# Two mixture-of-experts layers of a decoder: a streamed sort in the last one, and sorted expert tiles in the top-2 one

## The chip, the cores and the metric

The kernel runs on one core of one Trainium2 chip. The time is device microseconds of that core, from one execution; the number compared is the median over several executions. Each kernel also has one execution taken by the hardware profiler, whose span runs from the first to the last instruction.

## What is computed

Two decoder layers over 32 sequences of 128 tokens with 128 features (4096 tokens), all in float32: a bidirectional Mamba block, a cross attention, a top-2 mixture of experts; then a windowed attention, a cross attention and a top-1 mixture of experts. The change is in the two mixtures. The first, cut to what matters:

```
xt = layernorm(x).reshape(-1, 128);  logits = xt @ gate_w.T            # 8 experts
_, idx = top_k(logits + beta, 2);    probs = sigmoid(logits at idx)
c = zeros((4096, 8)).at[rows, idx].add(probs)
eo = for each expert: (silu(xt @ gate_e) * (xt @ up_e)) @ down_e       # inner width 256
x = x + sum_e c[:, e] * eo[:, e] + the same with the shared expert, weight 1
```

The last one: each token goes to the expert with the largest router logit, `gelu(x @ W1[e] + b1[e])` (inner width 512), then one common output matrix, the residual and a layernorm with its own gamma and beta.

## The kernel before

The six parts run one after the other; each has a block in which the five engines run their own lists of instructions and meet through semaphores. The tokens stay on chip in `S.x`, 128 tokens of a sequence on the partitions, and are worked on in `NG` = 8 groups of `GS` = 4 sequences (512 tokens). A part that needs weights of the next one issues their loads on SP's queue at its own start (`ahead.load(sp)`, L163).

**Top-2 layer** (`moe_top2_layer`, tiles named `c_`). A first block normalises all tokens (POOL's ten-step `ln_scalars`, then DVE), transposes them (L1301), forms the router's logits (L1305), splits the tokens and the expert weights into two parts `hi` and `lo` (L1322, L1325, L1381, L1392), and finds the two best experts of all 4096 tokens in one row of DVE steps (L1348 to L1379). A second block then runs every token through all 9 experts (8 and the shared one): 8 groups times 9 experts are 72 units. A unit is 4 projections of 128x512, each as three matmuls on the split parts (`split_pass`, L181 to L183), two Silu of 128x512 on ACT (L1465), two products on DVE (L1479), 8 output matmuls of 128x128 (L1443), and the weighted sum on DVE (L1503, L1505), where the weight is zero for the experts that a token did not choose.

**Top-1 layer** (`moe_top1_layer`, tiles named `f_`). A first block does the same preparation for all 4096 tokens (L1922, L1927, L1966), finds each token's expert, counts the tokens by expert with two matmuls and a scan, and works out each token's place in a sorted table in which each expert starts at a multiple of `TILE` = 256 (L1981 to L2025). Only then does POOL send the rows: 32 indirect DMAs, one for a sequence (L2048), into the DRAM table `f_sorted`, whose 6144 rows of 400 numbers were filled with blank rows beforehand. That fill is one DMA of 9600 KB, the last part of `moe_top1_weights`, issued on SP by the cross attention ahead of it:

```python
    blank = w["blank"].unsqueeze(0).to_broadcast([NT * TILE // 128, 128, ROW])
    W.part(W.sorted.rearrange("(j p) c -> j p c", p=128), blank)
```

A second block runs 24 tiles of 256 sorted tokens. For a tile SP loads the rows (L2078), PE transposes them (L2091) and multiplies by the one expert that the tile needs (L2101; ACT has copied its matrix, L2132, at an address read from the table `expert`) and by the output matrix (L2110), ACT does the Gelu (L2140), DVE the layernorm (L2151 to L2183), and POOL sends the rows to their tokens' places in the output with two indirect DMAs (L2206). ACT reads all 24 entries of `expert` ahead of its first tile (L2125).

The cross attention ahead of the top-1 layer loads for each sequence its context and mask on SP (L986, L993) a few sequences ahead, behind whatever SP issued before.

Of the kernel before, what the change touches and what calls it, by code (L numbers as in the profile page):

```python
# [24 lines left out]
GS = 4  # L25
# [1224 lines left out]

def moe_top2_weights(nc, ctx, w):
    W = Weights(nc, ctx, "cw_")
    W.router = W.tile("router", [128, E0], w["router"])
    W.bias = W.tile("bias", [128, E0], w["bias"].partition_broadcast(128))
    W.order = W.tile("order", [128, E0], w["order"].partition_broadcast(128))
    W.gu = W.tile("gu", [128, E0 + 1, 2, M0], w["gu"])
    W.down = W.tile("down", [128, E0 + 1, M0 // 128, D], w["down"])
    return W


def moe_top2_layer(nc, S, W, ahead):

    NE, MC = E0 + 1, M0 // 128
    BELOW = -1.0e38  # L1270
    with ExitStack() as ctx:
        A = Alloc(nc, ctx, "c_")
        gu_hi, gu_lo = (A.sb(n, [128, NE, 2, M0], F32R) for n in ("gu_hi", "gu_lo"))
        xh = [A.sb(f"xh{p}", [128, GS, D]) for p in range(2)]
        xT = [A.sb(f"xT{p}", [128, GT]) for p in range(2)]
        x_hi, x_lo = (A.sb(n, [128, NG, GT], F32R) for n in ("x_hi", "x_lo"))
        logits, sigm, sel, best, first, second, c = (
            A.sb(n, [128, NB, E0]) for n in ("logits", "sigm", "sel", "best", "first", "second", "c"))
        top, pick = A.sb("top", [128, NB]), A.sb("pick", [128, NB])
        with ExitStack() as ctx1:  # L1280
            B = Alloc(nc, ctx1, "c1_")
            pt = [B.ps(f"pt{k}", [128, GT]) for k in range(2)]
            pl = B.ps("pl", [128, NB, E0])
            s = {n: B.sem(n) for n in """rstd xh_ready t_mm xT_ready hi_ready lo_ready l_mm gu_hi_ready
                gu_lo_ready l_ready sigm_ready route""".split()}
            with nc.Block() as block:

                @block.sync
                def _(sp):
                    ahead.load(sp)  # L1290

                @block.tensor
                def _(pe):
                    pe.wait_ge(W.loaded, W.all())

                    def body(g, p):
                        pe.wait_ge(s["xh_ready"], g + 1)
                        if due(g - 1):
                            pe.wait_ge(s["xT_ready"], g - 1)
                        for i in range(GS):  # L1300
                            ins = nc.tensor.transpose(pt[p][:, i * T:(i + 1) * T], xh[p][:, i, :], S.ident[:, :])  # L1301
                        ins.then_inc(s["t_mm"], 1)
                        pe.wait_ge(s["xT_ready"], g + 1)
                        for i in range(GS):
                            ins = nc.tensor.matmul(pl[:, bass.ds(g * GS + i, 1), :], xT[p][:, i * T:(i + 1) * T],  # L1305
                                                   W.router[:, :], start=True, stop=True)
                        ins.then_inc(s["l_mm"], 1)
                    walk_groups(pe, body)

                @block.scalar  # L1310
                def _(act):
                    A_ = nc.scalar.activation

                    def body(g, p):
                        act.wait_ge(s["t_mm"], g + 1)
                        if due(g - 1):
                            act.wait_ge(s["l_mm"], g - 1)
                        if due(g - 1):
                            act.wait_ge(s["lo_ready"], g - 1)
                        A_(xT[p][:, :], pt[p][:, :], ACT.Copy).then_inc(s["xT_ready"], 1)  # L1320
                        act.wait_ge(s["xT_ready"], g + 1)
                        A_(x_hi[:, bass.ds(g, 1), :], bc(xT[p][:, :], 1, 1), ACT.Copy).then_inc(s["hi_ready"], 1)  # L1322
                    walk_groups(act, body)
                    act.wait_ge(W.loaded, W.all())
                    A_(gu_hi[:, :, :, :], W.gu[:, :, :, :], ACT.Copy).then_inc(s["gu_hi_ready"], 1)  # L1325
                    act.wait_ge(s["l_ready"], 1)
                    A_(sigm[:, :, :], logits[:, :, :], ACT.Sigmoid).then_inc(s["sigm_ready"], 1)

                @block.vector
                def _(dve):  # L1330
                    V = nc.vector
                    dve.wait_ge(s["rstd"], LN_STEPS)

                    def body(g, p):
                        if isinstance(g, int) and g == 1:
                            dve.wait_ge(s["rstd"], 2 * LN_STEPS)
                        if due(g - 1):
                            dve.wait_ge(s["t_mm"], g - 1)
# [46 lines left out]
                def _(pool):  # L1385
                    for part, cols in enumerate(LN_PARTS):
                        S.ln_scalars(pool, s["rstd"], LN_EPS, cols, part * LN_STEPS)
# [485 lines left out]
def moe_top1_layer(nc, S, W, out_d):  # L1873
# [9 lines left out]
    with ExitStack() as ctx:  # L1883
# [182 lines left out]
        def real(j):  # L2066

            return 0 <= j < NT
# [243 lines left out]
```

## Time and profile before

| | us |
|---|---|
| median of 3 runs | 2602.59 (2600.07 to 2607.44) |
| the profiled execution's own time | 2606.87 |
| its span, first to last instruction | 2605.1 |
| busy in the span: PE, DVE, ACT, POOL | 2228.4, 1960.4, 1402.3, 1305.2 |
| top-2 layer in the span | 1226.8 to 1610.1 |
| cross attention of the second layer | 2128.4 to 2393.3 |
| top-1 layer | 2393.9 to 2605.1 |

The shares of busy time are means over parts with different limits, so the table is only a frame: a part that changes is read in its own stretch. A row of the timeline gives the start, the duration, the engine, the line and the operation, and in brackets how long the engine had stood idle and what ended that.

### The profile page before, as it was taken

The numbers are of one execution on the slowest core, as the hardware profiler recorded it, in microseconds if no ns is written. First come the engines' busy times: TensorE is split into PE (matmuls) and PEld (weight loads), VectorE is DVE, ScalarE is ACT, GpSimd is POOL, SyncE is SP. The second block draws the span as 40 slices with busy tenths as digits, with TensorE's granted clock in tenths as the row PEclk, the third lists the DMA queues.
The fourth block names the chain that finished last, engine by engine and source line by source line (L and its number), as shares of the span: only waits on it lengthen the run. The fifth ranks groups of instructions, "written<-read, shape, count | busy, mean of one in ns | idle before, by whom it ended". The sixth has DMA issues, their size and how long they took to land. (4 is left out here: it accounts for less than half of the span.)

```text
span 2605.1 us, 45217 instructions
## 1 busy us (share of the span) xinstructions
PE 2228.4 (86%) x14292; PEld 1469.1 (56%) x14292; DVE 1960.4 (75%) x2979; ACT 1402.3 (54%) x2570; POOL 1305.2 (50%) x947
## 2 busy tenths in 40 slices
PE   4888888888888877998699997799999986998267
PEld 1344333334343335776588886566666654776266
DVE  5999999999999994776455555688888864777235
ACT  4666776665766644664322222566666643664044
POOL 4878887778887773333100002355555531233636
PEclk7999999999999998999699999899999987998589
DMA  4222222222222222001000000000000024000232
GB/s 119 74 75 73 75 72 70 76 70 75 76 74 70 73 65 67 12 11 27 1 1 1 0 0 6 1 0 0 0 0 0 0 82 124 12 12 5 92 116 78
DMA packets 79274, 116.20 MB, mean 45 GB/s; under 512 B 29124, under 2 KB 42611, under 8 KB 78464
## 3 DMA queue, kind: packets, MB, share of 16 engines
q1 hardware_dynamic: 75072, 105.76, 13.6%
q0 software_dynamic: 3584, 8.66, 0.9%
q8 instruction: 47, 0.77, 0.1%
q10 hardware_dynamic: 512, 0.53, 0.1%
q14 instruction: 59, 0.48, 0.1%
HBM read 105.73 MB, written 20.05 MB: 48 GB/s over the span
## 5 line engine op out<-in xcount | busy, mean ns | idle before, releaser
L858 POOL TENSOR_TENSOR m_hc<-m_h,m_cs 128x1024 f32<-128x1024 f32 x256 | 603.0, 2360 | 185.8 <-DVE m_h L768 167.6
L768 DVE TENSOR_TENSOR_SCAN m_h<-m_da,m_pdb 128x1024 f32<-128x1024 f32 x256 | 585.3, 2286 | 27.8 <-DVE m_pdb L740 3.9
L461 PE MATMUL m_py<-m_hc,ident 128*128 128x512 f32 x1024 | 508.9, 621 | 1.9 <-POOL m_hc L858 1.9
L643 ACT ACTIVATE m_da<-m_dt,m_aneg 128x508 f32<-128x508 f32 x512 | 331.9, 709 | 118.2 <-DVE m_h L768 102.6
L740 DVE TENSOR_TENSOR m_pdb<-m_du,m_pdb 128x1024 f32<-128x1024 f32 x256 | 309.1, 1208 | 29.4 <-PE m_pdb L448 20.3
L461 PEld LDWEIGHTS m_py<-m_hc,ident 128*128 128x128 f32 x1024 | 200.8, 199 | 225.2 <-issue 216.7
L1833 POOL TENSOR_TENSOR d_pr<-d_pr,d_rden 128x512 f32<-128x512 f32 x128 | 133.3, 1041 | 177.4 <-DVE d_rden L1764 177.4
L1465 ACT ACTIVATE c_act_of<-c_pg 128x512 f32<-128x512 f32 x144 | 86.2, 598 | 237.5 <-PE c_pg L183 237.5
L1111 ACT ACTIVATE x_prT<-x_pt 77x512 f32<-77x512 f32 x256 | 137.9, 587 | 132.1 <-PE x_pt L1013 131.2
L448 PE MATMUL m_pdb<-m_bcrow,m_sel 96*128 96x512 bf16 x256 | 102.0, 399 | 110.2 <-DVE m_h L768 110.2
L1227 POOL TENSOR_TENSOR x_kd<-x_kT,x_hm 128x308 f32<-128x308 f32 x64 | 45.1, 705 | 300.5 <-ACT x_v_raw L1123 300.5
L118 POOL TENSOR_TENSOR t<-bn 128x4 f32<-128x4 f32 (+1 forms) x4 | 1.0, 240 | 356.7 <-POOLq L66 356.5
L448 PEld LDWEIGHTS m_pdb<-m_bcrow,m_sel 96*128 96x128 bf16 x256 | 25.7, 100 | 227.4 <-DVE m_h L768 178.7
L1843 POOL TENSOR_TENSOR d_r<-d_mean_sq,minus_half 128x20 f32<-128x20 f32 x32 | 113.1, 3534 | 73.7 <-DVE d_mean_sq L1790 73.6
L1479 DVE TENSOR_TENSOR c_h<-c_act_of,c_pu 128x512 f32<-128x512 f32 x144 | 98.3, 687 | 63.4 <-PE c_pu L183 45.7
L1443 PEld LDWEIGHTS c_pd<-cw_down,c_h 128*128 128x128 f32 x1152 | 139.5, 191 | 5.5
L1443 PE MATMUL c_pd<-cw_down,c_h 128*128 128x128 f32 x1152 | 139.9, 275 | 0.0
L1013 PE MATMUL x_pt<-ident,x_pr 128*77 128x128 f32 x1024 | 139.4, 280 | 0.2
L1013 PEld LDWEIGHTS x_pt<-ident,x_pr 128*77 128x77 f32 x1024 | 117.7, 150 | 27.5 <-issue 24.8
L1600 PE MATMUL d_ps<-d_kT,d_qT 128*128 128x256 f32 x512 | 133.1, 383 | 0.0
L407 PE MATMUL m_pm<-m_xnT,m_wtap 128*128 128x512 f32 x256 | 124.2, 609 | 1.3 <-ACT m_xnT L558 1.3
L1173 DVE TENSOR_REDUCE x_top<-x_ps 128x8 f32<-128x616 f32 x128 | 101.9, 796 | 27.2 <-PE x_ps L1032 11.9
(269 smaller groups left out, 4895.4 us busy)
## 6 DMA issues: line engine op xcount, KB each, us to landing
m_cs<-crow SPq DMA_DIRECT2D x256, 256.0 KB, 3.1
f_sorted<-in_F_blank SPq DMA_DIRECT2D x1, 9600.0 KB, 39.3
f_row<-f_sorted SPq DMA_DIRECT2D x24, 400.0 KB, 3.5
cw_gu<-in_C_gu SPq DMA_DIRECT2D x1, 2304.0 KB
x<-in_x SPq DMA_DIRECT2D x8, 256.0 KB, 4.5
fw_w<-in_F_w SPq DMA_DIRECT2D x1, 2048.0 KB, 9.6
bm_mrow<-in_B_mrow SPq DMA_DIRECT2D x1, 1232.0 KB, 7.9
x_ctxT<-in_B_ctxT SPq DMA_DIRECT2D x32, 38.5 KB, 1.8
```

Source lines behind the costliest of these rows:

```text
L407: ins = mm(pm[1 - c][:, :], wtap[:, d, k, c * 128:(c + 1) * 128], xnT[:, par[0], :, off:off + T], start=k == 0, stop=k == TAPS - 1)
L448: mm(pdb[:, row_bank(n), :], sel[:, n, :], bcrow[d][:, :], start=True, stop=True).then_inc(s["b_mm"], 1)
L461: ins = mm(py[:, c, :], S.ident[:, :], hc[n % BUF][:, c, :], start=False, stop=n == NS - 1)
L643: A_(dst, src, ACT.Exp, scale=aneg[:, d, c, n:n + 1]).then_inc(s["da_ready"], 1)
L740: V.tensor_tensor(out, du[d][:, ::-1, :], bc(pdb[:, row_bank(n), :], 1, CH), ALU.mult).then_inc(s["db_ready"], 1)
L768: V.tensor_tensor_scan(h[n % BUF][:, way], da[n % BUF][:, d:d + CH * GT][:, way], pdb[:, b:b + 2, :].rearrange("p c t -> p (c t)")[:, way] ...
L858: P.tensor_tensor(hc[n % BUF][:, :, :], h[n % BUF][:, :].rearrange("p (c t) -> p c t", c=CH), bc(cs[n % BUF][:, :], 1, CH), ALU.mult).then ...
L1013: ins = tr(pt[e][0:TC, i * T:(i + 1) * T], pr[u.p][u.h][:, QH * e + i, :], S.ident[:, :])
L1111: A_(prT[u.p][Q2 * u.h + e][:, :], pt[e][0:TC, :], ACT.Copy).then_inc(s["prT_ready"], 1)
L1443: ins = mm(pd[k][:, i, :], h[k][:, c_, i * T:(i + 1) * T], W.down[:, e, c_, :], start=c_ == 0, stop=c_ == MC - 1)
L1600: ins = mm(ps[q % 2][:, 2 * k:2 * k + 2, :], qT[b.p][:, 2 * q + k, :], kT[b.p][:, q, :, :], start=False, stop=k == 1)
L1833: P.tensor_tensor(pr[qd][:, :, :], pr[qd][:, :, :], bc(rden[qd][:, :], 2, T), ALU.mult).then_inc(s["norm_ready"], 1)
```

## The change

1. **Top-1 layer, sort.** One block in place of two, and everything is done group by group: ACT normalises a group (with scale and shift, L2291) and copies its transpose, DVE adds the two residual columns (`fill`, before on POOL), chooses, and ranks the group against running counts (`rank`), and POOL sends the group's 4 sequences at once. To know a place before all tokens are counted, each expert has a region of its own, `REGION` = 4352 rows, in the DRAM table. The 9600 KB fill is gone; after the last group SP writes 256 blank rows behind each expert's last row (8 DMAs of 400 KB, at addresses read from `tail_at`), and reads each tile's address from `tile_at`. ACT reads the entries of `expert` one by one, two tiles ahead.
2. **Top-2 layer.** The same streamed sort, with rows of 144 numbers (128 features, and for each expert the weight and the destination), each token sent twice (64 indirect DMAs). During the sort the shared expert is computed densely: per group 4 plain float32 projections of 128x512, 2 Silu, 2 products, 8 output matmuls, one add into `S.x`. Then 40 tiles of 256 rows, each with its own expert's matrices (one copy of 128x768 on ACT), two indirect DMAs of the weighted rows into the DRAM table `c_routed`, and at the end 8 groups are read back, two tables of 256 KB each, and added to `S.x` (L109 statistics as before). The three-matmul split is gone: all matmuls are plain float32.

The other four parts are unchanged. The core of the diff:

```diff
-    W.gu = W.tile("gu", [128, E0 + 1, 2, M0], w["gu"])
-    W.down = W.tile("down", [128, E0 + 1, M0 // 128, D], w["down"])
+    W.gud = W.tile("gud", [128, E0 + 1, 3 * M0], w["gud"])
+    W.sorted = nc.dram_tensor("c_sorted", [E0 * REGION + TILE, ROW0], F32).ap()
+    W.routed = nc.dram_tensor("c_routed", [K0 * NB * T, D], F32).ap()
...
+                group(0)
+                logits(0)
+                for g in range(NG):
+                    shared(g, 0)
+                    if g + 1 < NG:
+                        group(g + 1)
+                    count_up(g)
+                    shared(g, 1)
+                    if g + 1 < NG:
+                        logits(g + 1)
+                    shared_down(g)
...
+                def weigh(g):
+                    act.wait_ge(r["raw_ready"], g + 1)
+                    into = rows[:, g * GS:(g + 1) * GS, D:ROW0].rearrange("p b (e w) -> p b e w", w=2)
+                    A_(into[:, :, :, 0], logit[:, :, :], ACT.Sigmoid).then_inc(r["sig_ready"], 1)
...
+                    if real(j + 1):
+                        e, k = e_of[j + 1], (j + 1) % KW
+                        A_(bc(wt[k][:, :], 1, 1), W.gud[:, bass.ds(e, 1), :], ACT.Copy).then_inc(s["w_ready"], 1)
...
+                for g in range(NG):
+                    choose(g)
+                    shared(g, 0)
+                    rank(g)
+                    if g + 1 == NG:
+                        tables()
+                    shared(g, 1)
+                    shared_add(g)
...
+                for g in range(NG):
+                    dve.wait_ge(routed_in[g % 2], 16 * K0 * (g // 2 + 1))
+                    V.tensor_tensor(seqs(S.x, g), seqs(S.x, g), back_in[g % 2][:, 0], ALU.add).then_inc(s["half_ready"], 1)
...
+                    for b in range(g * GS, (g + 1) * GS):
+                        for k in range(K0):
+                            P.indirect_dma_start(W.sorted, bass.IndirectOffsetOnAxis(slot_of[:, k, b:b + 1], 0),
+                                                 rows[:, b, :], None).then_inc(sorted_in, 16)
...
-    W.sorted = nc.dram_tensor("f_sorted", [NT * TILE, ROW], F32).ap()
-    blank = w["blank"].unsqueeze(0).to_broadcast([NT * TILE // 128, 128, ROW])
-    W.part(W.sorted.rearrange("(j p) c -> j p c", p=128), blank)
+    W.blank = w["blank"]
+    W.sorted = nc.dram_tensor("f_sorted", [E1 * REGION + TILE, ROW], F32).ap()
...
+                for e in range(E1):
+                    at = sp.value_load(tail_at[0:1, e:e + 1], min_val=e * REGION, max_val=e * REGION + NB * T)
+                    sp.dma_start(W.sorted[bass.ds(at, TILE)], W.blank).then_inc(blank_in, 16)
...
-                e_of = [act.value_load(expert[0:1, j:j + 1], min_val=0, max_val=E1 - 1) for j in range(NT)]
```

SP's queue in the second cross attention, where the loads for the top-1 layer stand between the context loads of the first two sequences and those of the third (`x_ctxT`, `x_mask`). Before:

```order
L986 DMA x_ctxT<-in_E_ctxT 128x77
L993 DMA x_mask<-in_E_mask 128x77
...
L163 DMA fw_w<-in_F_w 128x4096
L163 DMA fw_wo<-in_F_wo 128x512
L163 DMA f_sorted<-in_F_blank 48x4x12800
...
L986 DMA x_ctxT<-in_E_ctxT 128x77
```

And now:

```order
L163 DMA fw_beta<-in_F_beta 128x128
L163 DMA fw_w<-in_F_w 128x4096
L163 DMA fw_wo<-in_F_wo 128x512
L997 UNCONDITIONAL_BRANCH
...
L986 DMA x_ctxT<-in_E_ctxT 128x77
...
L993 DMA x_mask<-in_E_mask 128x77
```

The fill of `f_sorted` no longer stands ahead of the third sequence's context.

PE in the top-2 layer of the changed kernel: first a group of the sort (`c_gT` is the group's transpose, `c_ones` and `cw_above` count), then a tile (`c_wt` holds the tile's expert):

```order
L1413 MATMUL c_pg<-c_gT,cw_gud 128x512
L1414 MATMUL c_pu<-c_gT,cw_gud 128x512
L1384 MATMUL c_pt<-ident,c_rows 128x128 x4
L1402 MATMUL c_pu<-c_chosen,c_ones 128x32
L1403 MATMUL c_pu<-c_chosen,cw_above 128x32
L1413 MATMUL c_pg<-c_gT,cw_gud 128x512
L1414 MATMUL c_pu<-c_gT,cw_gud 128x512
L1392 MATMUL c_pg<-cw_router,c_gT 128x8 x4
L1423 MATMUL c_pd<-cw_gud,c_sh_h 128x128 x8
...
L1446 MATMUL c_pt<-ident,c_row 128x128 x2
L1463 MATMUL c_pg<-c_xT,c_wt 128x256 x2
L1468 MATMUL c_pu<-c_xT,c_wt 128x256 x2
```

A group holds one expert's projections where a group before held nine, and a tile takes 256 rows through one expert; the tile ends with 4 output matmuls of 128x128 (L1481).

ACT in a group of that sort, with the loads of its function tables:

```order
L1501 ACTIVATE c_rows<-x,c_nmr,c_rstd 128x128 x4
L1515 ACT_TABLE_LOAD
L1515 ACTIVATE c_rows<-c_logit 128x4x8
L1522 ACT_TABLE_LOAD
L1522 ACTIVATE c_sh_act<-c_pg0 128x512
L1510 ACTIVATE c_gT0<-c_pt0 128x512
L1522 ACTIVATE c_sh_act<-c_pg0 128x512
```

Two table loads stand in each of the 8 groups, where the layer before had two in all.

## Rows read from the trace of the kernel before

**Rows 1.** Windows: us of each stretch, busy of PE, PEld, DVE, ACT, POOL, then clock.

```profile
1226.80:1279.20 52.40, 22.86 (x96) 19.54 (x97) 21.27 (x48) 15.46 (x20) 20.46 (x28) 0.50 0.08 27
1279.20:1610.10 330.90, 328.54 (x2016) 292.99 (x2016) 188.35 (x448) 87.42 (x145) 0.00 (x0) 0.99 0.00 1
2393.90:2436.20 42.30, 24.80 (x100) 20.55 (x100) 33.13 (x87) 4.78 (x8) 27.65 (x22) 0.50 0.00 1
...
960.00:976.00 16.00, 11.51 (x28) 4.29 (x26) 15.55 (x10) 2.28 (x4) 11.43 (x5) 1.00 0.17 44
```

**Rows 2.** Waits in 2130 to 2200: who waited for whom, us, times, longest.

```profile
PE x_pqkv L1042 <- DMA x_ctxT<-in_E_ctxT: 29.5, 1, 29.5
```

**Rows 3.** DMA issues of the page: count, KB each, us to landing.

```profile
f_sorted<-in_F_blank SPq DMA_DIRECT2D x1, 9600.0 KB, 39.3
x<-in_x SPq DMA_DIRECT2D x8, 256.0 KB, 4.5
```

**Rows 4.** Timeline of POOL in the top-1 layer's sort, first and last of 32.

```profile
2436.19 1.22 POOL L2048 DMA_INDIRECT f_sorted<-f_rows,f_slot_of  x1 [13.22 <-DVE f_slot_of L2018]
...
2475.74 0.96 POOL L2048 DMA_INDIRECT f_sorted<-f_rows,f_slot_of  x1 [0.30 <-issue]
```

**Rows 5.** Timeline from the top-1 layer's first row load to its first projection.

```profile
2481.91 36.22 SPq L2078 DMA_DIRECT2D f_row<-f_sorted  x10
2485.05 0.29 PEld L2091 LDWEIGHTS f_pt<-ident,f_row 128*128 128x128 f32 x2 [53.88 <-DMA f_row<-f_sorted]
...
2495.19 0.38 ACT L2131 ACTIVATE f_xT<-f_pt 128x256 f32<-128x256 f32 x1 [69.84 <-issue]
...
2496.23 3.75 PE L2101 MATMUL f_pi<-f_xT,f_w 128*128 128x256 f32 x8 [9.40 <-ACT f_w L2132]
```

**Rows 6.** Timeline of PE, one tile of the top-1 layer at full clock.

```profile
2507.59 0.38 PE L2091 MATMUL f_pt<-ident,f_row 128*128 128x128 f32 x2
2507.81 1.89 PE L2101 MATMUL f_pi<-f_xT,f_w 128*128 128x256 f32 x8
2509.54 1.95 PE L2110 MATMUL f_py<-fw_wo,f_gelu 128*128 128x128 f32 x16
2511.32 0.38 PE L2091 MATMUL f_pt<-ident,f_row 128*128 128x128 f32 x2
```

**Rows 7.** Timeline of PE at half clock: 4 logits, two projections of 128x512.

```profile
2400.86 1.87 PE L1927 MATMUL f_pl<-fw_router,f_xT 128*128 128x8 f32 x8 [0.69 <-ACT f_xT L1948]
...
1617.02 3.37 PE L1636 MATMUL d_pq<-dw_wq,d_xT 128*128 128x512 f32 x4 [0.45 <-ACT d_xT L1701]
```

**Rows 8.** Timeline of ACT: table load, sigmoid, 4 scaled copies, copy of 128x256, Silu.

```profile
1269.36 1.28 ACT L1327 ACT_TABLE_LOAD   x1
1270.66 0.42 ACT L1327 ACTIVATE c_sigm<-c_logits 128x256 f32<-128x256 f32 x1
...
10.16 1.65 ACT L529 ACTIVATE m_xh<-x,m_mr,m_r 128x128 f32<-128x128 f32 x4
...
2508.01 0.38 ACT L2131 ACTIVATE f_xT<-f_pt 128x256 f32<-128x256 f32 x1 [1.06 <-PE f_pt L2091]
...
1280.87 0.60 ACT L1465 ACTIVATE c_act_of<-c_pg 128x512 f32<-128x512 f32 x1 [0.41 <-PE c_pg L183]
```

**Rows 9.** Timeline of DVE: two dependent small steps, one product, four statistics.

```profile
2433.30 0.17 DVE L2003 TENSOR_TENSOR_SCAN f_end<-f_ones,f_tiles 128x8 f32<-128x8 f32 x1
2433.51 0.17 DVE L2006 TENSOR_TENSOR f_start<-f_end,f_tiles 128x8 f32<-128x8 f32 x1
...
1282.23 0.69 DVE L1479 TENSOR_TENSOR c_h<-c_act_of,c_pu 128x512 f32<-128x512 f32 x1 [3.81 <-PE c_pu L183]
...
1609.24 0.87 DVE L109 BATCH_NORM_STATS2 bn<-x 128x6 f32<-128x128 f32 x4
```

**Rows 10.** Instructions on two tiles: duration ns min/median/max, first and last start.

```profile
L2206 POOL DMA_INDIRECT out_x<-f_done,f_row x48: 969/976/1106, 2510.2 to 2595.7; - x48
...
L1966 DVE TENSOR_SCALAR f_rows<-x,f_mv,f_rstd x32: 329/587/1370, 2397.8 to 2420.3; 128x128 f32<-128x128 f32 x32
```

More of the change, by code:

```diff
@@ L1272, in moe_top2_layer @@
         A = Alloc(nc, ctx, "c_")
[L1273 to L1279, printed above, removed]
@@ L1416, in moe_top2_layer @@
-        with nc.Block() as block:
+        rows = A.sb("rows", [128, NB, ROW0])
+        mv = A.sb("mv", [128, NB, 2])
+        ve, rstd, nmr = (A.sb(n, [128, NB]) for n in ("ve", "rstd", "nmr"))
+        gT = [A.sb(f"gT{p}", [128, GT]) for p in range(2)]
+        logit, rival, best, best2, first, second, chosen, moved, based, mine = (
+            A.sb(n, [128, GS, E0]) for n in
+            ("logit", "rival", "best", "best2", "first", "second", "chosen", "moved", "based", "mine"))
+        top, pick, place = (A.sb(n, [128, GS]) for n in ("top", "pick", "place"))
@@ new lines, in moe_top2_layer @@
+        keep, upto = (A.sb(n, [128, E0, GS]) for n in ("keep", "upto"))
+        ones = A.sb("ones", [128, 128])
+        run = [A.sb(f"run{k}", [128, E0]) for k in range(2)]
+        count, tiles, end = (A.sb(n, [128, E0]) for n in ("count", "tiles", "end"))
+        full = A.sb("full", [128, E0, NM])
+        past, spent = (A.sb(n, [128, NT, E0]) for n in ("past", "spent"))
+        which, skipped, from_, base = (A.sb(n, [128, NT]) for n in ("which", "skipped", "from", "base"))
+        slot_of = A.sb("slot_of", [128, K0, NB], I32)
@@ L1866, in moe_top1_weights @@
     W.wo = W.tile("wo", [128, M1 // 128, D], w["wo"])
[L1867 to L1869 removed]
+    W.blank = w["blank"]
+    W.sorted = nc.dram_tensor("f_sorted", [E1 * REGION + TILE, ROW], F32).ap()
     return W
@@ new lines, in moe_top1_layer @@
+        rows = A.sb("rows", [128, NB, ROW])
+        mv = A.sb("mv", [128, NB, 2])
+        ve, rstd, nmr = (A.sb(n, [128, NB]) for n in ("ve", "rstd", "nmr"))
+        gT = [A.sb(f"gT{p}", [128, GT]) for p in range(2)]
+        best, chosen, moved, based, mine = (A.sb(n, [128, GS, E1]) for n in ("best", "chosen", "moved", "based", "mine"))
+        top, pick, place = (A.sb(n, [128, GS]) for n in ("top", "pick", "place"))
+        keep, upto = (A.sb(n, [128, E1, GS]) for n in ("keep", "upto"))
@@ new lines, in moe_top1_layer @@
+        ones = A.sb("ones", [128, 128])
+        run = [A.sb(f"run{k}", [128, E1]) for k in range(2)]
+        count, tiles, end = (A.sb(n, [128, E1]) for n in ("count", "tiles", "end"))
+        full = A.sb("full", [128, E1, NM])
+        past, spent = (A.sb(n, [128, NT, E1]) for n in ("past", "spent"))
+        which, skipped, from_, base = (A.sb(n, [128, NT]) for n in ("which", "skipped", "from", "base"))
+        slot_of = A.sb("slot_of", [128, NB], I32)
+        expert, tile_at = (A.sb(n, [128, NT], I32) for n in ("expert", "tile_at"))
@@ L2147, in add @@
+                dve.wait_ge(r["const"], 4)
+                fill(0)
+                for g in range(NG):
+                    choose(g)
+                    if g == 0:
+                        shift(2, PARTS[2])
+                    if g + 1 < NG:
+                        fill(g + 1)
+                    rank(g)
+                tables()
                 def add(j):
```

1002 lines of the change are left out of this document (627 added, 375 removed).

## The prediction, made before the run

> **What bounds the kernel now.** I read the windows first: they cut the span into the stretches that the change touches and say which engine fills each. In the top-2 layer PE is busy 328.5 of 330.9 us at a clock of 0.99 [rows 1]: nothing but less work for PE shortens it. It follows 52.4 us of preparation at half clock, so the layer takes 383.3 us. In the top-1 layer PE leads only once the tiles run. Before that come 42.3 us of preparation, 40.5 us in which only POOL's 32 sends run [rows 4], and 19.5 us, to 2496.2, in which nearly nothing runs [rows 5]: 102.3 us from the layer's start to its first projection. The waits show a third place, in a part whose code is not edited: in the second cross attention PE stood 29.5 us for a context load [rows 2]. In the list of DMA issues the reader sees why: the fill of the sorted table, 9600 KB, took 39.3 us to land [rows 3], and that context load was issued behind it.
>
> **Term 1, the fill goes: -29.** SP's queue keeps 2.5 MB of weights ahead of the third sequence's context, but not the fill. At the fill's own rate, 9600 KB in 39.3 us, those weights need some 10 us from 2134, so the context is there by about 2145, when PE asked for it. The stall goes but for about a microsecond: -29. Bounds: 0 if another load is late in its place, -33 if the climb of the clock after the stall is saved too.
>
> **Term 2, the top-1 layer's sort: -38.** Each POOL send takes (2475.74 - 2436.19) / 31 = 1.28 us [rows 4]; 4 make a group, 5.1 us. Nothing else in a group is longer. PE at half clock, where this stretch stays [rows 1]: 4 transposes, 0.9 by twice the tile's pair at half the speed [rows 6], the logits 1.87 [rows 7], and two small counting matmuls of about 0.3, 3.4 us. DVE: 12 small dependent steps at 0.21 and two adds of 0.69 [rows 9], 3.9 us. ACT: 1.65 + 0.60 [rows 8], 2.3 us. So POOL sets the pace and the 40 us of sends cover the rest. The first group is placed after about 14 us: statistics and a power step 2, scaled copies 1.65, transposes 1, copy 0.6, logits 1.9, the counting behind the next group's 3.6, DVE's steps and fills 3. Then 8 x 5.1 = 41, some 3 for the landing (bounds: the 1.0 of the next send and the 5.2 us from the last send's end to SP's first load, which hold a barrier too [rows 4, 5]), 1 for SP's read of an address and its issue, 3.1 from issue to PE's first transpose [rows 5], 0.4 for ACT's copy: 63, say 64. The tails, 8 blank DMAs, are 3.2 MB, 13 us at the fill's rate [rows 3], and SP may start them 10 us before the last send: they end about with it; if not, they cost up to 6. ACT's 24 table reads, now ahead of its first copy, fill most of 2481.9 to 2495.2 [rows 5], 0.55 us each; in the change only one stands there. So 102.3 becomes 64: -38, bounds -32 and -42. The 24 tiles keep their 3.73 us [rows 6]: ACT gets one read of 0.55 us more per tile beside two copies and four Gelus, 0.38 + 0.60 [rows 8] and about 1.6, still under PE.
>
> **Term 3, the top-2 layer: 383.3 to 267, -116.** (a) To the first group's place 15 us, as above with more steps on DVE. (b) A group: POOL sends 8 times, 10.2 us. DVE has about 26 small steps of 0.21, two products and an add of 0.69, and a wait for the shared expert's 8 output matmuls (8 x 0.22 [rows 6]): 9.4. ACT has 1.65, two table loads, each followed by its function 1.30 after its start, 0.2, two Silu and a copy of 0.60 [rows 8]: 6.3. PE has 4 projections of 128x512: the pair took 3.37 at half clock [rows 7], so 6.7, or 3.4 at full; with transposes, logits, counts and output matmuls 13.8 at half and 6.9 at full. At half clock PE would set about 15 us, at full POOL 10.2. I take full: a scan stretch in which PE was busy 11.5 of 16 us held 1.00 [rows 1], and here it would be busy 6.9 of 10.2 with no gap over 2 us; the stretches that stayed at 0.50 have only transposes and 8-column matmuls. 8 groups: 82. (c) Landing, read of the address, load: 7. (d) 40 tiles. PE: transposes 0.22, 4 matmuls of 128x256 1.73, 4 of the 8 output matmuls 0.89 [rows 6]: 2.84. ACT: weight copy of 768 columns 0.82 (0.60 for 512 and 0.22 for each 256 more [rows 8]), 0.38, 0.60, 0.2 for two columns, the read 0.55: 2.6. POOL: two sends, 2.6. DVE: 0.69 + 2 x 0.34 + 0.15: 1.5. PE leads, closely; with hand-offs I take 3.1, so 124, and 2 for a first tile at half clock (3.75 against 1.73 [rows 5, 6]). Bounds: 2.84 and 3.6. (e) From PE's last tile to its rows landed: 7. (f) Reading back: DVE adds twice and takes statistics, 2 x 0.69 + 0.87 [rows 9], but with two buffers a group waits for SP's issue, a landing of 4.5 [rows 3] and the adds of the group two before: (0.9 + 4.5 + 1.4) / 2 = 3.4, with the start 30. Sum: 15 + 82 + 7 + 126 + 7 + 30 = 267.
>
> The Trainium skill (ScalarE: Activation LUTs, "What ACT_TABLE_LOAD costs") puts a change of table at about 2.66 us with its drain and says to batch calls by set, which this change does not do. By it ACT's group would be 9.0 us, still under POOL's 10.2, and since DVE waits for ACT once in a group the sum would be some 3 us higher, by my estimate. The rows show 1.30 from a load's start to its function's [rows 8], and the sum goes by that.
>
> **Sum.** -29 - 38 - 116 = -183 on the profiled execution's own 2606.9 us: 2424. That execution was 4 us above the median of the runs shown, so the median may lie nearer 2420; hand-offs between engines that I have left out go the other way. Forecast: **2425 us**.
>
> **Rivals.**
> - *Half clock in the top-2 sort* (15%): PE sets 15.0 us a group, + 8 x 4.8 = 38: 2463. For it: the sort starts cold, and each group waits on a chain through DVE. Against: at half clock PE would be busy 13.8 of 15, which no row at 0.50 with wide matmuls keeps for long.
> - *ACT sets the tiles* (9%): if a table read inside the running stream costs what it does not alone, a tile takes 3.6 and the sum is + 20: 2445.
> - *The stall stays* (8%), held by the 2 MB of weights: + 29, 2454. Against: 2.5 MB is a quarter of the fill.
> - *Sends slow down beside a busy DVE* (7%). In the sort before DVE stood idle while POOL sent, now it is 90% busy. If a send's 0.97 us becomes 1.7, as DVE's own 128x128 steps took 0.59 beside POOL's adds where their least was 0.33 [rows 10], a send takes 2.0: 64 of them + 47, 80 (4.0 a tile in place of 3.1) + 36, 32 + 23: 2531. Against it: the last layer's sends took 0.97 to 1.11, 0.98 in the middle, in a tile loop with DVE at work [rows 10]. The Trainium skill (SBUF — State Buffer, "SBUF: two separate sides") says that descriptors made on GpSimd wait while VectorE runs a two-port operation; most steps here are of kinds that it does not name, and the rows decide.
> - *Tiles one after the other* (3%), the slower side. The 40 tiles gain only while a tile's chain overlaps the next. In series it is: read 0.55, weight copy 0.8, transposes and copy 0.6, projections 1.7, Silu 0.6, product 0.69, output 0.9, weighting 0.7, two sends 2.6, landing 2.4: 12 us. If a buffer (three `done`, three `wt`, four `row`) ties a tile's start to the end of the one before, 40 x 12 = 480 in place of 124: 2780, slower than now. The change turns slower from 3.1 + 183/40 = 7.7 us a tile. Against: in the top-1 layer the same scheme ran at PE's pace [rows 6].
>
> **How the numbers follow.** My forecast's case has 58%. Its own range is 2402 to 2440 by the bounds above. Half clock, ACT's pace and the stall that stays lie within 2470; beyond it are slower sends, the serial tiles and sums of two rivals, some 15%; below 2402 perhaps 4%. Range: 2402 to 2470. A measurement of this kernel can tell about 0.3%, 8 us. All cases but the serial tiles, and combinations near them, end below 2595: faster 96%, same 1%, slower 3%.
>
> **What would show it.** Right: in the second cross attention no DMA wait near 2145; POOL's sends 1.28 apart through both sorts, with a gap at most at group boundaries; clock near 1.00 from the second group of the top-2 sort on; tiles 3.1 apart with PE busy over 90%; first projection of the top-1 layer 64 us after its start. Wrong: group periods of 15 us at 0.50; ACT busy without idle in the tiles; sends of 1.5 us or more beside DVE; the read-back longer than 40 us; or a new wait of ten or more microseconds for tail blanks or row loads. The forecast falls as a whole if any tile period is over 4 us.

## The result, and the profile after

The changed kernel takes 2477.44 us (2469.95 to 2484.33, 4 runs) where the kernel before takes 2604.29 (2600.07 to 2607.44, 4 runs): ratio 0.951, 95% interval 0.948 to 0.955. It is faster, by 127 us and not by 180: 52 us above the forecast of 2425, and 7 above the upper end of its range. The profiled execution is the shortest of the four: 2469.95 us with a span of 2468.2. Three executions of the experiments, one of them of the kernel before, took 4215 to 5274 us and are left out of the medians below.

First the windows, with the columns of [rows 1], of the stretches that the forecast had priced: the top-2 layer's preparation, its sends, its tiles; the last layer's preparation, its sends, and from the last send to the first projection.

```profile
1225.50:1241.10 15.60, 11.01 (x38) 7.41 (x39) 9.43 (x69) 9.86 (x19) 6.16 (x3) 0.60 0.31 99
1241.10:1350.80 109.70, 66.50 (x284) 44.35 (x282) 48.20 (x209) 39.52 (x63) 61.52 (x64) 0.77 0.15 50
1358.90:1489.00 130.10, 119.42 (x699) 106.32 (x700) 50.54 (x150) 69.45 (x158) 71.61 (x73) 0.95 0.28 78
2280.30:2294.40 14.10, 8.29 (x36) 7.12 (x36) 8.97 (x64) 7.26 (x18) 6.88 (x6) 0.50 0.10 30
2294.40:2340.00 45.60, 21.50 (x94) 19.22 (x94) 23.84 (x105) 10.51 (x25) 31.82 (x32) 0.50 0.45 159
2340.00:2356.80 16.80, 1.21 (x5) 0.81 (x6) 0.00 (x0) 1.01 (x2) 0.00 (x0) 0.50 0.72 231
```

Two rows stand out. The 64 sends of the top-2 layer last 109.7 us, in which no engine is busy for more than 66.5; I had given them 82. And the last row is a stretch in which nothing computes and the DMA engines move 231 GB/s.

The waits in 1225 to 1350, columns as in [rows 2], say whom the sends wait for:

```profile
POOL c_sorted L1769 <- DVE c_slot_of L1652: 39.2, 6, 10.5
...
PE c_pu L1402 <- DVE c_chosen L1620: 30.8, 4, 13.2
DVE x L1665 <- remote: 32.1, 3, 13.2
ACT c_rows L1515 <- DVE c_logit L1587: 31.2, 5, 13.8
```

POOL, PE and ACT all wait for DVE, and DVE for "remote", which is the trace's word for a releaser that it can't name. The timeline of all engines in the longest of these stops shows what DVE was waiting for by the program:

```profile
1320.08 2.05 PE L1423 MATMUL c_pd<-cw_gud,c_sh_h 128*128 128x128 f32 x16
...
1322.83 1.02 PE L1414 MATMUL c_pu<-c_gT,cw_gud 128*128 128x512 f32 x2
...
1329.53 0.96 POOL L1769 DMA_INDIRECT c_sorted<-c_rows,c_slot_of  x1 [0.30 <-issue]
1333.27 0.69 DVE L1665 TENSOR_TENSOR x<-x,c_pd 128x512 f32<-128x512 f32 x1 [13.25 <-remote]
```

The addition to `x` needs the shared expert's output in `c_pd`. PE's 16 matmuls for it ended at 1322.1 and PE had gone on to the next group's, yet DVE started at 1333.3, 11.1 us late. POOL went on sending meanwhile, a send every 1.26 us and each 0.96 long: it is not the sends that are slowed, but the engines beside them. The trace also holds the times at which semaphores were raised. The one that this addition waits for was raised at 1333.24, 0.03 us before DVE started and 11.1 after the matmuls' end; at the other three stops of this kind it is the same (0.02 or 0.03 us before DVE's start, and 8.4, 4.3 and 3.5 after the matmuls' end). So it is the signal that came late by the trace, and not DVE's own instruction.

It is the same in the last layer's sort. The matmuls that count end at 2318.6 and the transposes at 2319.5; DVE and ACT, which wait for one each, start 4.4 and 3.5 us later and within 0.06 us of each other.

```profile
2318.00 0.61 PE L2237 MATMUL f_pi<-f_chosen,fw_above 128*128 128x32 f32 x2
...
2318.43 1.09 PE L2218 MATMUL f_pt<-ident,f_rows 128*128 128x128 f32 x4
...
2322.98 0.22 DVE L2377 TENSOR_TENSOR_SCAN f_upto<-f_keep,f_pi 128x32 f32<-128x32 f32 x1 [7.81 <-remote]
2323.04 0.60 ACT L2299 ACTIVATE f_gT<-f_pt 128x512 f32<-128x512 f32 x1 [5.72 <-remote]
```

I call this a stop: an engine stands still though what it waits for is over by the trace.

The other places. The second cross attention takes 234.1 us from its first context load to the last layer's start, where it took 265.8, at a clock of 0.96 for 0.90; the row of [rows 2] has no successor. The first line is of before, the second of after:

```profile
2128.40:2394.20 265.80, 226.98 (x3232) 175.72 (x3232) 168.98 (x357) 139.24 (x320) 68.17 (x132) 0.90 0.19 57
```

```profile
2046.20:2280.30 234.10, 224.78 (x3232) 174.32 (x3232) 168.89 (x357) 139.83 (x320) 68.01 (x133) 0.96 0.09 23
```

In the last layer the first send starts at 2294.38, 14.1 us after the layer's start, and the last at 2339.04 (for [rows 4]). Then the answer to [rows 5]:

```profile
2333.45 13.14 SPq L2194 DMA_DIRECT2D f_sorted<-in_F_blank  x8
...
2339.04 0.96 POOL L2512 DMA_INDIRECT f_sorted<-f_rows,f_slot_of  x1 [0.30 <-issue]
2350.85 8.79 SPq L2204 DMA_DIRECT2D f_row<-f_sorted  x8
...
2356.76 3.62 PE L2262 MATMUL f_pi<-f_xT,f_w 128*128 128x256 f32 x8
```

SP issues the eight blanks in 13.1 us, the last behind the last send, and the first row is loaded 10.9 us after that send's end. The first projection comes 76.5 us after the start of the layer. The tiles keep their 3.73 us of [rows 6]:

```profile
2375.43 0.38 PE L2251 MATMUL f_pt<-ident,f_row 128*128 128x128 f32 x2
...
2379.16 0.38 PE L2251 MATMUL f_pt<-ident,f_row 128*128 128x128 f32 x2
```

### The profile page after: what moved, and what is told of

Its sections match the earlier page's. It is cut to its first block and busy times, and to the rows that moved or that the text cites. A ratio compares the mean times of both kernels' runs of the same rounds, so it can differ in the third digit from the quotient of the medians.

```text
span 2468.2 us, 43398 instructions
## 1 busy us (share of the span) xinstructions
PE 2078.3 (84%) x13248; PEld 1323.3 (54%) x13248; DVE 1879.3 (76%) x3049; ACT 1431.6 (58%) x2678; POOL 1410.2 (57%) x1050
## 5 line engine op out<-in xcount | busy, mean ns | idle before, releaser
L448 PEld LDWEIGHTS m_pdb<-m_bcrow,m_sel 96*128 96x128 bf16 x256 | 25.5, 100 | 228.7 <-DVE m_h L768 183.8
L1775 POOL DMA_INDIRECT c_routed<-c_done,c_to x80 | 78.6, 983 | 71.1 <-DVE c_done L1738 47.2
L1159 DVE RECIPROCAL x_rden<-x_pyo 128x128 f32<-128x128 f32 x64 | 61.3, 957 | 70.4 <-PE x_pyo L1067 70.4
L1179 DVE TENSOR_TENSOR x_pr<-x_ps,x_top 128x616 f32<-128x616 f32 x128 | 102.3, 800 | 14.1
L1943 ACT ACTIVATE d_cT<-d_py 128x256 f32<-128x256 f32 x128 | 49.1, 384 | 108.6 <-PE d_py L1873 107.8
L2012 DVE TENSOR_REDUCE d_den<-d_pr 128x4 f32<-128x512 f32 x128 | 87.1, 681 | 29.7 <-ACT d_pr L1949 29.2
```

What stands on the lines that cost most here:

```text
L448: mm(pdb[:, row_bank(n), :], sel[:, n, :], bcrow[d][:, :], start=True, stop=True).then_inc(s["b_mm"], 1)
```

## The experiments

They ran on five chips, called by their numbers here, each beside the kernel before on the same chip; the medians of that one are 2603.8 to 2607.9. Each chip had one set of runs only. A result without a ratio is from a single execution.

**The unchanged kernel again, its two halves, and the overlap taken away (chip 5).**

> The changed kernel once more, unchanged. In its first profile DVE stood still for 12.4, 6.4, 13.3 and 7.4 us at the addition to x of groups 1, 3, 6 and 7 of the top-2 sort, and for 7.8 us at the scan of group 3 of the top-1 sort, with no other engine named as what ended it, though TensorE's last matmul for it was over. Theory A, the instructions of an engine come late at fixed places of the unrolled program: the stops stand at the same groups, with about the same lengths, and the sends of the top-2 layer last 109 us again. Theory B, TensorE's signals or DVE's start are held up by the sends that run beside them: stops of the same kind and of 25 to 60 us in all, but at other groups and of other lengths, so that the sends last anything from 95 to 125 us. Theory C, one disturbed execution: no stops, and the sends last 82 to 90 us.

Measured: 2474.88. Stops at the addition in groups 1, 3, 5 and 7, of 12.4, 10.7, 11.9 and 8.3 us, and sends over 112.6 us. POOL and DVE at the ends of the first two stops:

```profile
1262.22 0.96 POOL L1769 DMA_INDIRECT c_sorted<-c_rows,c_slot_of  x1 [0.30 <-issue]
1265.78 0.69 DVE L1665 TENSOR_TENSOR x<-x,c_pd 128x512 f32<-128x512 f32 x1 [12.43 <-remote]
...
1293.30 0.95 POOL L1769 DMA_INDIRECT c_sorted<-c_rows,c_slot_of  x1 [0.30 <-issue]
1296.35 0.69 DVE L1665 TENSOR_TENSOR x<-x,c_pd 128x512 f32<-128x512 f32 x1 [10.67 <-remote]
```

Theory C falls. All four stops here ended 2.1 to 2.6 us after the last of 16 sends, about a send's landing. Between the two eights of such a row POOL stands idle for 0.3 to 1.5 us, but each time before the matmuls' end, so these gaps don't show whether so short a one would end a stop. Other groups than in the first profile, but the first stop is the same to 0.01 us; A is not out by this run.

> The streamed sort of the last layer alone, with the top-2 layer as it was before. My working gave 29 us for the fill that is no longer issued in the second cross attention, and the profile after shows 76.5 us from the start of the last layer to its first projection where it was 102.3, so 26 us: 29 + 26 = 55 us less, 2549 us. If the stall in the cross attention did not really go, 2578; if the last layer gains the 38 us that I had forecast, 2537.

> The sorted top-2 layer alone, with the last layer and its fill as they were before. The profile after shows 300.5 us for the top-2 layer where it was 383.3: 83 us less, 2521 us. If the layer costs the 267 us of my forecast when the rest is as before, 2488. If the parts add, this saving and that of the last layer alone make up the whole of the change's 127 us, within the 14 us by which its own runs differ.

The first is a kernel with the layer and tables of before for the top-2 experts, the second one with those of before for the last layer. Measured: 2550.84 (ratio 0.978, 0.976 to 0.980) and 2534.93 (0.972, 0.971 to 0.974). Against that chip's 2607.47 they save 56.6 and 72.5 us, in sum 129; the whole change saved 133 there (2474.88). The parts add. The second stands 14 us above the 2521 expected: the top-2 layer lasts 307 us in its profile (1225.5 to 1532.4), where it took 300.5 in the first profile, and the rest of the 14 was not followed up. In the first the second cross attention lasts 234.0 us too: the fill's stall is gone with it, whatever the top-2 layer does. The last layer has stops in it as well (4.8 and 6.4 us of DVE).

> The changed kernel, in which POOL starts its sends only when the last place of the layer is known, in both sorts; nothing else differs. This takes the overlap of sends and computing away. Theory B (the sends hold up the signals beside them): no stop over 2 us stands in either sort, the top-2 groups follow one another in 10 to 12 us, the 64 sends take 64 x 1.26 = 81 us behind them, and the kernel is 50 to 60 us slower, about 2535. Theory A (instructions come late): the stops stay, 30 to 40 us in the top-2 sort, and it is 80 to 90 us slower, about 2560.

```
-                for g in range(NG):
+                pool.wait_ge(r["place_ready"], K0 * K0 * NG)
+                for g in range(NG):
                     pool.wait_ge(r["xh_ready"], g + 1)
```

and the same in the last layer. Measured: 2529.51, and no stop in either sort. The window is from the first place to the last:

```profile
1242.00:1313.60 71.60, 58.23 (x276) 38.08 (x275) 45.30 (x200) 40.01 (x65) 0.00 (x0) 0.92 0.00 1
```

Seven groups in 71.6 us, 10.2 each, at a clock of 0.92, beside a DMA share of 0.00. The same instructions on the same chip, with sends beside them, had four stops. So the stops need the sends beside them: theory B, and A falls, since the program of DVE, PE and ACT is the same here. The 2529.51 us are near the 2535 of theory B.

**Pauses between sends, and blanks on two queues (chip 0).**

> The changed kernel, in which the eight tail blanks of the last layer are issued by SP and by ACT's queue in turns, four each, where SP issued all eight one behind the other (8 x 1.64 = 13.1 us, the last 4 us before the first load of a sorted row). My theory: the start of the last layer's tiles waits for the blanks, and their issue takes half of that wait: the first row load comes 4 to 7 us earlier, and the kernel takes 2470 instead of 2477. Rival, the 3.2 MB set it and not the issue: at the 244 GB/s of the old fill (9.6 MB in 39.3 us) they last 13 us from the first one on whoever issues them, and 1 us or less is gained. Rival, the end of the sends sets it: nothing changes.

```
-                for e in range(E1):
+                for e in range(0, E1, 2):
                     at = sp.value_load(tail_at[0:1, e:e + 1], ...
...
+                act.wait_ge(r["table_ready"], 1)
+                for e in range(1, E1, 2):
+                    at = act.value_load(tail_at[0:1, e:e + 1], ...
+                    act.dma_start(W.sorted[bass.ds(at, TILE)], W.blank).then_inc(blank_in, 16)
```

> The changed kernel, in which POOL waits in both sorts before every fourth send until all the sends before it have landed. Theory B1 (TensorE's signals are held up while a long row of sends runs without a pause, and come through when it has landed, since in the repeated profile every stop ended 2.0 to 2.6 us behind the end of a row of 16 sends): no stop over 5 us is left; each pause costs POOL 2 us, so the sends of the top-2 layer last 64 x 1.26 + 15 x 1.5 to 2 = 103 to 111 us, and the kernel takes what it did, 2465 to 2485. Theory B2 (a send holds them up by itself, however many there are): the stops stay about as long in sum, the pauses come on top where POOL is the one waited for, 2490 to 2510.

> The same with the wait before every eighth send, so at every group of the top-2 sort and every second one of the top-1 sort. Theory B1: the stops of 8 to 12 us shrink to under 5 us, since a row of sends is never longer than 10.1 us; the sends last 8 x (10.1 + 2) = 97 us in place of 110, and the kernel takes 2460 to 2470. Theory B2: nothing shrinks, 2480 to 2495.

```
+                            n = K0 * b + k
+                            if n and n % 8 == 0:
+                                pool.wait_ge(sorted_in, 16 * n)
                             P.indirect_dma_start(W.sorted, ...
```

(with 4 in the first of the two, and by `b` in the last layer)

> The changed kernel, in which a send starts only when the last but one before it has landed, so that at most two are under way; the two take turns in two semaphores. Landing took 2.4 to 2.6 us for a send and one follows the other in 1.26, so POOL hardly waits. Theory B1 in the form that a backlog of sends holds the signals up: there is none then, no stop over 2 us, sends in 82 to 95 us, 2450 to 2460. Theory B1 in the form that POOL's own unbroken making of sends does it: the stops stay unless the waits open gaps of some tenths of a us, 2475 to 2485.

```
+                            if b:
+                                pool.wait_ge(sorted_in[k], 16 * b)
                             P.indirect_dma_start(W.sorted, ...
-                                                 rows[:, b, :], None).then_inc(sorted_in, 16)
+                                                 rows[:, b, :], None).then_inc(sorted_in[k], 16)
```

Measured: 2414.29 (0.926, 0.925 to 0.928), 2455.45, 2434.41 (0.936, 0.932 to 0.939) and 2432.62. None of the four has a stop in a sort, not even the first, which changes nothing in the top-2 layer. That could not come from the edits, and no unchanged kernel had run beside them to compare with, which was a mistake. The only one of the four without pauses is the two-queue kernel. Against it the pauses at every eighth send cost 20 us and those at every fourth 41, with the blanks' second queue in the difference; the sends of both sorts take 11.7 and 11.0 us longer in the profile of the first, 23.1 and 20.8 in that of the second, which covers it. The windows of the two-queue kernel, for the second, third and fifth row shown of after:

```profile
1253.40:1335.80 82.40, 63.02 (x284) 42.58 (x283) 49.45 (x210) 39.63 (x63) 61.59 (x64) 0.88 0.20 70
1340.30:1453.00 112.70, 112.14 (x691) 103.05 (x692) 51.49 (x150) 68.13 (x158) 70.77 (x72) 0.97 0.32 89
...
2256.10:2297.80 41.70, 21.49 (x94) 19.21 (x94) 24.08 (x105) 10.51 (x24) 32.23 (x32) 0.50 0.56 202
```

Here the sends take 82.4 and 41.7 us, my 82 and 41, and in the tiles PE is busy without a gap.

**Program or chip (chip 13).**

> The changed kernel unchanged, as the control that the last four runs lacked: in all four no stop of DVE over 2 us stood beside the sends, also in the top-2 layer of the kernel whose only edit is in the last layer (its blanks on two queues), which took 2414 where 2470 was expected. Theory P, the stops belong to the program: the unchanged one has them again, 35 to 45 us of them in the top-2 sort, and takes 2470 to 2484. Theory Q, they belong to the chip or to the time of the run, and the last four ran where there are none: the unchanged kernel has none either and takes about 2425 to 2435, so that my edits of POOL's waits had nothing to remove.

> The kernel with the tail blanks on two queues, unchanged, beside the control. Theory P: 2410 to 2422 again, with no stops, while the control has them. Theory Q: as far below the control as the blanks are worth, 4 to 15 us, with or without stops as the control.

> The changed kernel with four more register loads on ACT ahead of the last layer's tiles (the ones that the two-queue kernel needs), and all blanks on SP's queue as before. If the stops went in the two-queue kernel because its instructions or semaphores lie otherwise in the program (theory P, form 1), they go here too: 2430. If ACT's queue for transfers or the blanks themselves did it (P, form 2), the stops stand: 2470 to 2484. Theory Q: as the control, within 2 us.

```
+                act.wait_ge(r["table_ready"], 1)
+                for e in range(1, E1, 2):
+                    act.value_load(tail_at[0:1, e:e + 1], ...
```

> Both edits together: the blanks on two queues, and POOL waits for all sends to land before every eighth. If the pause is what takes stops away where they are, and costs its 8 x 2 us where POOL is the one waited for: at most 2425 on any chip, and 2420 to 2430 where the two-queue kernel alone has no stops. If the two-queue kernel is free of stops by itself, the pauses only cost: 8 to 16 us slower than it.

Measured: 2476.32 (0.949, 0.947 to 0.951), 2478.76 (0.950, 0.948 to 0.952), 2483.79 (0.953, 0.951 to 0.955), 2459.71 (0.944, 0.942 to 0.946). The two-queue kernel, instruction for instruction the one that took 2409.80 to 2422.07 on chip 0, takes 2474.45 to 2480.45 here, and its profile has the stops back (12.3 and 12.1 us among them). Its windows of the same two stretches of the top-2 layer:

```profile
1247.20:1354.60 107.40, 63.04 (x281) 42.26 (x280) 48.40 (x209) 39.46 (x63) 61.96 (x64) 0.80 0.14 47
1367.80:1498.00 130.20, 115.91 (x682) 102.25 (x683) 49.16 (x146) 68.21 (x154) 69.17 (x71) 0.97 0.27 77
```

PE's 63.0 us of work in the sends are the same; the stretch is 25 us longer. So theory Q: 64 us between two chips for one program, while the kernel before differs by 4 (2603.83 and 2607.93). Theory Q leaves open whether it is the chip or the time of the run, and so do these runs. The four register loads on ACT took no stop away either (12.7 and 12.2 us among those left), and that kernel is 7.5 us slower than the unchanged one, where Q allowed 2; this was not explained. With the blanks on two queues the first row is loaded 8.2 us after the end of the last send, where the unchanged kernel here has 12.7; that is the 4 to 7 us that the first expectation on the blanks had given, but the time shows nothing of it (2.4 us more than the unchanged kernel, within the spread). Q was wrong in one thing: my edits of POOL's waits do have something to remove. With the pause at every eighth send one stop of 4.6 us is left in the top-2 sort, and the kernel is 19 us faster than without it; "at most 2425 on any chip" was wrong by 35, since the tiles (below) stay slow.

**Backlog or unbroken row (chip 14).**

> The changed kernel unchanged, once more as the control, since the chip decides: with stops on two chips (2475 and 2480), while four edited kernels had none on a third, where the unchanged one was not run. Where the profile shows no stop over 2 us in the top-2 sort, it takes 2425 to 2440 by the two-queue kernel's 2414 there and the 10 us that the blanks held up the last layer; where it shows 35 to 45 us of stops, 2470 to 2484.

> POOL waits for all sends to land before every eighth, blanks as in the change. Where the control has stops: 15 to 25 us less than it, since most of them go and the sends of the top-2 layer last 93 us in place of 108 (as with the two-queue kernel, 2460 against 2479). Where it has none: 5 to 15 us more than it, by the 8 pauses.

> At most two sends under way, in both sorts. If a backlog of sends holds the signals up, this does better than the pause at every eighth where the control has stops: no stops, the top-2 sends in 88 us as on the chip without stops, 20 to 30 us less than the control. If an unbroken row of sends does it and not their number in flight, the stops stay and it takes what the control does. Where the control has none, within 5 us of it or up to 10 us slower, since the last layer's larger sends lasted 54.7 us this way on the chip without stops, where the two-queue kernel had 40.7.

> The same with the last layer's tail blanks on two queues: within 3 us of it, since the slower sends of the last layer then end last and hide the blanks (they were issued 15 us before the last send in the two-out kernel). If the blanks still end last, 4 us less.

Measured: 2478.86 (0.952, 0.950 to 0.955), 2456.45 (0.942, 0.940 to 0.944), 2475.63 (0.951, 0.949 to 0.953), 2474.66 (0.951, 0.948 to 0.954). The unchanged kernel has 38 us of stops in the top-2 sort here. The rows show two of POOL's seven pauses in the top-2 sort of the second kernel, then two of DVE's stops in the third:

```profile
1260.69 0.96 POOL L1772 DMA_INDIRECT c_sorted<-c_rows,c_slot_of  x1 [2.13 <-DMA c_sorted<-c_rows,c_slot_of]
...
1272.63 0.96 POOL L1772 DMA_INDIRECT c_sorted<-c_rows,c_slot_of  x1 [2.13 <-DMA c_sorted<-c_rows,c_slot_of]
```

```profile
1269.78 0.69 DVE L1666 TENSOR_TENSOR x<-x,c_pd 128x512 f32<-128x512 f32 x1 [7.35 <-remote]
...
1313.79 0.69 DVE L1666 TENSOR_TENSOR x<-x,c_pd 128x512 f32<-128x512 f32 x1 [12.00 <-remote]
```

A pause of 2.13 us every 11.9 leaves two stops of 4.7 and 4.9 and brings the 64 sends to 93.7 us, 17 less than the unchanged kernel's 110.6 (1244.1 to 1354.7). With at most two sends under way, stops of 7.4, 12.0 and 5.2 are left, 24.5 us in sum where the unchanged kernel has 38.1, and the sends take 105.1. The number in flight is at most a part of it, then; what helps most of what was tried is that POOL stops for the length of a landing. The two-out kernel also slows the last layer's sends to 55.3 us for 32, so that the blanks are hidden, and the fourth kernel stands 1 us below the third, within the spread.

**The unchanged kernel on one more chip (chip 11).**

> The changed kernel unchanged, one look on whatever chip comes. With stops beside the sends (35 to 45 us in the top-2 sort) it takes 2470 to 2486. Without any, 2420 to 2440: then the missing stops of the third chip were the chip's doing alone, and the forecast of 2425 holds there.

Measured: 2481.31, with stops of 12.1, 12.4 and 8.2 us. So the unchanged kernel was never seen without them.

## Why the prediction was right, and where it failed

The terms against the two profiled executions: -31.7 for the second cross attention, -25.8 for the last layer up to its first projection, -82.8 for the top-2 layer (1225.5 to 1526.0, 300.5 us), and +3.4 elsewhere, in sum the 136.9 by which the spans differ.

- **Term 1, -29: right.** 265.8 to 234.1. The context that PE had waited for comes in time, and the clock that the stall had cost is saved too, which was the bound of -33. It comes without the top-2 layer as well (2550.84).
- **Term 2, -38: came to -26.** The first place after 14.1 us was right (14), and the tiles' 3.73. The 8 groups took 45.6 in place of 41, for stops of 2.9 and 7.8 us on DVE, where chip 0 gave 41.7. The other 8 us are the blanks, which I had end about with the last send, at a cost of 6 if not. The stops are in this too: they hold back DVE's table of tail places, and SP can't issue before it. Where the pauses take the stops away, SP issues the blanks at 2316.3 to 2327.9, before the last send, and the first row is loaded 1.9 us after that send's end (chip 14) in place of 10.9.
- **Term 3, -116: came to -83, and its step (b) is where the forecast failed.** (a) 15.6, forecast 15. (b) "8 groups x 10.2 = 82": 109.7. Every duration in it held. Sends start 1.26 apart, each 0.96 long beside a busy DVE; a group without sends beside it goes by in 10.2 us; and on chip 0 all 64 take 82.4. What failed is the tacit step that engines which share no resource in the trace run side by side at their own pace. The price of the hand-offs beside the sends stood in the sum at nothing, and in the first profile DVE stood for 39.5 us in four stops, where 2.1 is its usual wait at this addition. (c) 8.1, forecast 7. (d) and (e), first transposes to last row stored: 141.6, forecast 133; chip 0 took 124.3 (1340.3 to 1464.6), with PE at 2.84 us a tile, the lower bound, where 3.25 stand here. The 3.25 is a mean: in the first profile too the median tile takes 2.84. POOL's stores of finished tiles run beside the computing in this stretch, and short stops for "remote" stand in it on the chips that have the long ones (up to 3.6 us of ACT in the first profile, where PE's signal came 2.2 us after its matmuls' end); that they are the whole difference is argued and was not tested. (f) 25.5, forecast 30: the landing was 3.3 us where I had 4.5.

The rivals. *Half clock* is wrong in its reason: with no sends beside it a group takes 10.2 at 0.92, so PE does not set it. The granted clock was 0.77 in the 109.7 us, where PE stands through the stops, and 0.88 and 0.92 where there are none (chip 0, and the late sends). *ACT sets the tiles*: no, on chip 0 PE is busy 112.14 of 112.70. *The stall stays*: no. *Sends slow down beside a busy DVE*: no, 0.96. It was the nearest in kind and had the direction wrong: not the sends wait for the computing, but the computing for the sends. The Trainium skill (SBUF — State Buffer, "SBUF: two separate sides"), which I had weighed for it, tells of DMA descriptors held up on GpSimd's side, and of one of VectorE and GpSimd blocking the other for the length of an instruction; nothing here shows either, since the sends kept their 0.96 us, and the stops last up to 13.3 us and stand on ACT as well. *Tiles in series*: no. Among the signs I had listed as wrong was a new wait of ten or more microseconds for tail blanks, and it is there, 10.9.

The change of table on ACT cost what [rows 8] show, 1.29 us from the load's start to the Silu's in the top-2 sort of after:

```profile
1264.90 1.28 ACT L1522 ACT_TABLE_LOAD   x1
...
1266.19 0.60 ACT L1522 ACTIVATE c_sh_act<-c_pg 128x512 f32<-128x512 f32 x1
```

By the Trainium skill (ScalarE: Activation LUTs, "What ACT_TABLE_LOAD costs") it would be 2.66, about 1.28 for the load, as here, and the rest for a drain, which does not show in these rows; the measurement decides, and in the kernel with late sends ACT's two changes a group fit into 10.2 us.

The range ended at 2470 because I had put beyond it only slower sends, serial tiles and sums of two rivals. A case "something in the overlap itself costs" stood in none of them, though overlap was the whole of the change. The chances of the sign held: 0.96 for faster.

**What stays open.** What makes the signals late was not settled. The stops need sends beside the computing; a pause of POOL of 2.1 us at every eighth keeps most of them away; on chips 5, 13, 14 and 11 they came in every kernel whose sends ran beside the computing without such pauses, the first always at the addition of group 1 of the top-2 sort, 12.1 to 13.6 us long where the sends were left as in the change; on chip 0 they came in none of four. Whether the unchanged kernel would be free of them on chip 0 was not measured; the two-queue kernel is, and it stood within 2.4 us of the unchanged one on chip 13. No run tells POOL's making of a send from the packets that the send sets off.

One rival stands untested, that the recording takes part. Each of the 64 sends of the top-2 sort raises its semaphore 16 times, 1024 in all. The trace of the two-queue kernel on chip 0 holds all 1024 of these, that of the same kernel on chip 13 holds 238, and the first profile 241: on the chips with stops a part of the record is missing at the sends. It is missing too where the sends run late and nothing computes beside them (172 in that trace), so the gaps in the record don't come from the stops. That the signals themselves are held up and that the recording holds them up both fit this. Each execution here is listed with a granted clock, so none can be called free of recording, and a run without it was not made.

**The best of these kernels** is the change with POOL's wait at every eighth send: 2456.45 on chip 14, where the change took 2478.86 and the kernel before 2606.99 (2453.20 to 2457.30 against 2478.19 to 2486.75, four runs each). With the blanks on two queues it took 2459.71 on chip 13, against 2476.32. On chip 0, without stops, the pauses cost: 2434.41 with them, 2414.29 for the two-queue kernel without.

## What to carry to other kernels

When a change gains by letting POOL's indirect sends run beside the computing, price the hand-offs between the other engines too, and look in the trace for engines that start long after what releases them. A wait for landing before every eighth send is a break of 2.1 us in the top-2 sort; the kernel was 19 and 22 us faster with it where there were such stops, and 20 us slower than the two-queue kernel where there were none. And run the unchanged kernel beside every set of experiments, on the same chip: here one program differed by 64 us between two chips, more than any edit of the sends was worth.

## What the hardware showed that I had not expected

- Signals came late beside a long row of sends on four chips of five. DVE stood for up to 13.6 us at one addition (chip 14); of the 13.3 us shown above, 11.1 lay behind the end of PE's matmuls. In the last layer DVE and ACT, released by signals due 0.9 us apart, started 0.06 apart. It is not PE's signals alone: in the two-queue kernel on chip 13, PE's output matmuls, which wait for DVE's product, started 2.1 us after its end, and DVE's signal for them was raised 0.04 us before that start.

```profile
1349.09 0.68 DVE L1660 TENSOR_TENSOR c_sh_h<-c_sh_act,c_pu 128x512 f32<-128x512 f32 x1
...
1351.84 3.79 PE L1423 MATMUL c_pd<-cw_gud,c_sh_h 128*128 128x128 f32 x16 [8.47 <-remote]
```

- The chip, or the occasion, matters where sends and computing overlap, and hardly in the kernel before: 2414.29 against 2478.76 for one program, 2603.83 against 2607.93 for the kernel before.
- At most two sends under way stretched the 32 sends of the last layer to 55.7 us, where they took 41.7 unhindered; the top-2 layer's, with rows of 576 bytes in place of 1600, went from 82.4 to 89.3 (chip 0).
